# Attention: value pass in whole 512-column blocks instead of 256-column pieces, one block every second half step

## The reference, cut to what matters

```python
B, T, E = x.shape                      # 4, 1024, 128
q, k, v = ...                          # each (B, T, 16, 8); q and k are rotated
scores = jnp.einsum('bqhd,bkhd->bhqk', q, k) * scale
pages = jnp.arange(T) // PAGE_SIZE     # PAGE_SIZE = 32
allowed = pages[None, :] <= pages[:, None]
scores = jnp.where(allowed[None, None], scores, jnp.finfo(scores.dtype).min)
attn = jax.nn.softmax(scores, axis=-1)
out = jnp.einsum('bhqk,bkhd->bqhd', attn, v).reshape(B, T, E)
return out @ wo
```

## Time and profile before

| what | value |
|---|---|
| median of three runs | 1579.98 us |
| the profiled execution, its own time | 1579.82 us |
| its span in the profile | 1578.0 us |
| attention's value pass runs | from 142.0 us to about 486 us of the span |
| between 201.37 and 438.44 us: TensorE busy | 229.95 of 237.07 us |
| VectorE busy there | 232.91 us |
| ScalarE busy there | 221.52 us |

### The profile page before, as it was taken

One profiled execution on the slowest core, in us unless ns is written; L12 is line 12 of the kernel. 1 busy time (PEld: TensorE's weight loads), 2 busy tenths in 40 slices (PEclk: granted clock), 3 DMA queues, 4 the chain that ended last, 5 costly groups with the idle time before them and its releaser, 6 DMA issues. The chain is left out here.

```text
span 1578.0 us, 23831 instructions
## 1 busy us (share of the span) xinstructions
PE 1248.7 (79%) x7728; PEld 585.0 (37%) x7728; DVE 1171.5 (74%) x1342; ACT 727.4 (46%) x1121; POOL 506.3 (32%) x371
## 2 busy tenths in 40 slices
PE   4917999999985679999978767667666766666998
PEld 2402333333333534444533212222222222246565
DVE  5838999999954534444456789999999999984444
ACT  2504999999994143333336763323323323302221
POOL 2310001011002212233242256667666766622000
PEclk9956999999997579999988869999999999995999
DMA  3321111111104200000010022212212212100000
GB/s 89 137 74 36 64 45 54 51 56 57 37 21 118 68 0 1 0 0 0 0 27 0 4 69 80 79 58 76 80 66 76 70 66 80 53 1 27 14 13 27
DMA packets 45554, 74.01 MB, mean 47 GB/s; under 512 B 8983, under 2 KB 24999, under 8 KB 45479
## 3 DMA queue, kind: packets, MB, share of 16 engines
q1 hardware_dynamic: 44776, 72.26, 14.1%
q10 hardware_dynamic: 702, 0.73, 0.2%
HBM read 59.47 MB, written 13.11 MB: 46 GB/s over the span
## 5 line engine op out<-in xcount | busy, mean ns | idle before, releaser
L1586 POOL TENSOR_TENSOR ms_ch<-xnT,ms_c_rows 128x1024 f32<-128x1024 f32 x128 | 307.8, 2406 | 156.9 <-DVE xnT L1555 130.1
L611 DVE TENSOR_REDUCE att_found<-PS 128x2 f32<-128x1024 f32 (+2 forms) x288 | 333.4, 1219 | 19.9 <-PE PS L690 17.9
L666 ACT ACTIVATE att_prob<-PS 128x512 f32<-128x512 f32 x576 | 313.4, 596 | 28.3 <-PE PS L712 15.3
L1555 DVE TENSOR_TENSOR_SCAN xnT<-ms_decay,PS 128x1024 f32<-128x1024 f32 x128 | 285.2, 2269 | 0.0
L1533 ACT ACTIVATE ms_decay<-m_dt,m_a 128x1024 f32 x128 | 146.7, 1148 | 300.2 <-DVE xnT L1555 300.2
L1495 PE MATMUL PS<-ms_ch,ident_sb 128*128 128x512 f32 x512 | 265.3, 644 | 5.9 <-DVE m_u L1561 3.3
L1488 PE MATMUL PS<-m_bc,m_w_sel_b 96*128 96x512 bf16 (+1 forms) x256 | 83.9, 413 | 149.7 <-DVE xnT L1555 142.5
L731 PE MATMUL PS<-att_prob,att_v 128*32 128x256 f32 (+1 forms) x2560 | 182.2, 371 | 3.0 <-ACT att_out L655 2.8
L1550 DVE TENSOR_TENSOR PS<-ms_dtu,PS 128x1024 f32<-128x1024 f32 x128 | 150.9, 1215 | 16.0 <-PE PS L1488 15.6
L690 PE MATMUL PS<-kr,qr 55*128 55x128 bf16 (+4 forms) x1152 | 121.0, 291 | 41.4 <-DMA qr<-page_q 27.6
L1495 PEld LDWEIGHTS PS<-ms_ch,ident_sb 128*128 128x128 f32 x512 | 105.2, 207 | 101.8 <-issue 78.0
(11 more groups left out here) (209 smaller groups left out, 1594.1 us busy)
## 6 DMA issues: line engine op xcount, KB each, us to landing
ms_c_rows<-c_rows_dram SPq DMA_DIRECT2D x64, 512.0 KB, 3.6
qk_parts_dram<-qkv_parts SPq DMA_DIRECT2D x48, 128.0 KB, 1.8
heads_dram<-att_out SPq DMA_DIRECT2D x16, 256.0 KB, 2.5
qr<-qk_parts_dram SPq DMA_DIRECT2D x32, 96.0 KB
qr<-qk_parts_dram SPq DMA_DIRECT2D x96, 32.0 KB
kr<-qk_parts_dram SPq DMA_DIRECT2D x96, 32.0 KB
kr<-qk_parts_dram SPq DMA_DIRECT2D x32, 96.0 KB
X<-x SPq DMA_DIRECT2D x4, 512.0 KB, 6.0
```

What stands on the lines that cost most here:

```text
L611: dve.tensor_reduce(found[:, :, pair, first:first + (n - 1) * step + 1:step], PS[:, bank:bank + 2, :].rearrange("p r (w n) -> p r w n", w= ...
L666: act.activation(prob[:, step % PROB_RING * GH + h, :], PS[:, SCORE_BANK + unit % SCORE_RING, :], ACT.Exp, scale=float(D) ** -0.5).then_in ...
L1555: dve.tensor_tensor_scan(h[:, k, half, :], decay[:, k, half, :], inputs(half), 0.0, ALU.mult, ALU.add).then_inc(scanned, 1)
L1586: pool.tensor_tensor(ch[:, half, :], h[:, r % 2, half, :], c_rows[:, r, :], ALU.mult).then_inc(ch_ready, 1)
```

## The change

The pieces become whole blocks: 9 of 512 columns. Block v comes behind the scores of half step 2v + 4 (for v below 4) or 2v + 3.

```diff
@@ -448,7 +448,7 @@
 TURN_K = 7
-PIECE = 256
+PIECE = BANK
 NV = NK * BANK // PIECE
@@ -465,7 +465,7 @@
 def due(v):
 
-    return v + 4 if v < NV // 2 else v + 3
+    return 2 * v + 4 if v < NV // 2 else 2 * v + 3
```

## The result

The changed kernel takes 1624.8 us (median of four runs, 1619.9 to 1631.6) against 1580.2 for the kernel before on the same chip: a ratio of 1.0284, 95% interval 1.0238 to 1.0329. That is slower by 44.6 us; the forecast was 1622, 42 slower. Its profiled execution took 1628.7 us, with a span of 1626.9.

The account below looks back on a forecast made before the run. No engine was taken as full: TensorE, VectorE and ScalarE hand work to each other, with a ring floor of 1.08 us. About +2.8 us a group, 42.3 over the whole, took 1580.0 to 1622; range 1608 to 1633 for 8 in 10.

Parts of the forecast that it names:

- widening, nine half steps: Half steps going from one piece to two pieces' columns cost 0.43 us each, +3.87 a group; a vanishing wait gives -0.09.
- six emptied half steps: Half steps 0, 2, 5, 7, 9 and 16 lose their piece, falling only from 1.12 to 1.08 us: -0.24 a group.
- half step 12: It loses its double visit and falls from 1.55 to 1.08 us: -0.47 a group.
- half step 14: Without its piece the turn comes early, but ScalarE's copy waits behind an exponential: 1.60 to about 1.35 us, -0.25.
- behind the last turn: With no maxima left, 11 widened half steps cost +2.9 us and one losing a double visit gives -0.26: +2.6.
- first group: Half steps 4 to 7, at 1.2 GHz, cost +0.4 us; half steps 8 to 14 cost +1.0.
- the ring's floor: Scores wait for an earlier exponential in the ring of three banks, so no half step is shorter than 1.08 us.
- VectorE's floor: VectorE needs 21.2 us a group at most for 18 half steps, which no change of TensorE's order can pass.
- the bounds of the visit's length: A visit of 512 columns costs 0.86 to 1.14 us, taken as 1.00; 20 us either way in all.
- the first (TensorE's saved time counts): Faster: 8 fewer visits a group at 0.14 us, stopped by VectorE's 21.2 us, give 1574 us; chance 4%.
- The second: No change: empty half steps give back what long ones take, pairs of 2.24 us, 1580 us; chance 3%.
- The third: Slower still: TensorE's idles make the granted clock fall at times in the stage, eight falls, 1632 us; chance 8%.

Follow-up runs that it names:

- three pairs: The kernel before with pieces 2, 4 and 6 moved one half step later: 1603.8 us, ratio 1.0134.
- The old and the filled tail: Changed kernel, last two groups in the order before: 1618.5 us; or with unread maxima matmuls in those groups' half steps without a visit: 1627.7 us.
- copy first: Kernel with 18 spread pieces and early turn, plus the second group's copy DMAs moved ahead of the fourth group's row loads: 1579.1 us, ratio 0.9982.

## Why the prediction was right

Its range, direction and mechanism held, and the bulk of its sum did. The first four rows are the terms of one group and add up to the fifth; the last five rows above the sum are those of the whole stage. Both columns are differences of the changed kernel from the one before, the right one in the profiled executions:

| term | forecast, us | measured, us |
|---|---|---|
| widening, nine half steps | +3.87 - 0.09 = +3.78 | +3.73 |
| six emptied half steps | -0.24 | -0.19 |
| half step 12 | -0.47 | -0.41 |
| half step 14 | -0.25 | -0.21 |
| a group | +2.8 | +2.92 |
| twelve intervals of turns | 33.6 | 34.8 |
| second group | 2.2 | 2.2 |
| interval before the last turn | 2.5 | 2.6 |
| behind the last turn | 2.6 | 7.3 |
| first group | 1.4 | 2.4 |
| sum of the last five | 42.3 | 49.3 |

The span itself grew by 48.9 us: 0.7 us come before the first turn and about 1 less behind the last visit. That the median of 1624.8 lies within 3 us of the forecast of 1622 is partly luck. The profiled run has 6.6 us over my 42.3, and two of the four runs, 1619.9 and 1620.8, lie under the forecast.

The visit was read rightly from the double one, and the ring's floor from the single empty half step. A size was off: I took 1.08 us for every empty half step. The odd-numbered ones (3, 5, 7, 9) take 1.06 to 1.08, the even-numbered ones (0, 2, 12, 16) 1.12 to 1.14, and so do 6, 8 and 10 with three pairs. The difference lies between the scores and their exponential: it starts 0.42 us behind its scores in half step 5 (294.88 to 295.30) and 0.47 in half step 2 (290.88 to 291.35). Why isn't shown. It makes most of the 1.2 us between 33.6 and 34.8.

Two statements of the prediction were wrong without moving its number. VectorE's floor was 21.05 and not 21.2, as said above. And the bounds of the visit's length don't both stay in the range: by its own 20 us either way they give 1602 and 1642, and the range was 1608 to 1633. The measured 1.00 us kept this from mattering.

The rivals: the first (TensorE's saved time counts) needed empty half steps under 0.69 us, and they took 1.07. The time saved in the visits is real, though: one visit takes 1.00 us where two took 1.14. The Trainium skill, "TensorEngine Tiling (Array Packing)", Key Properties, says that a change of the tiling mode drains the engine, and this trace agrees in sign; no run tells how much of the 0.14 us is the drain. ScalarE's hold of the ring took this gain and more. The second needed a ring wait of 0.1 us; rows after an idle of ScalarE show 0.47.

The third was placed wrongly, and it is most of what the profiled run has over my sum. I asked for the clock in the stage, where it stays at 1.00 with TensorE 82% busy, and reasoned with that share. I had worked out the last group without maxima for its length and not for its share: 0.32 + 1.00 + 0.32 us in a pair of 2.42, some 68%. There the clock fell, for 13.7 us. So one sign that I had named for being wrong, a fall of the clock, did come, outside the stage that I had it watched in:

```profile
514.14 0.61 PE L712 MATMUL PS<-qr,kr 51*128 51x512 bf16 x2
515.44 0.61 PE L712 MATMUL PS<-qr,kr 51*128 51x512 bf16 x2 [0.69 <-ACT att_prob L666]
515.98 1.93 PE L731 MATMUL PS<-att_prob,att_v 128*32 128x512 f32 x8
517.85 0.61 PE L712 MATMUL PS<-qr,kr 51*128 51x512 bf16 x2
```

A pair of half steps takes 3.70 us there (514.14 to 517.85) instead of the 2.47 of this group at 1.00, so 13.7 x (1 - 2.47 / 3.70) = 4.6 us, which is about the 4.7 between 7.3 and 2.6.

The first group's extra 1.0 is the clock too: it rose at 154.2 us in the changed kernel and at 149.7 in the kernel before. This one is chance as far as the runs tell. The old and the filled tail have the same order in the first group, and there the clock rose at 149.4 and 149.3 us, and the first interval of turns took 25.92 and 25.88 us instead of 27.33.

## What to carry to other kernels

When several engines hand work to each other through a shallow ring, look for the shortest interval that the ring allows before work is bunched: time taken out of a step that is already at this floor is lost, and time put into its neighbour is paid in full. The trace of before may have one odd step of each kind, as here, and two such steps are worth more than any average. Look at the granted clock in every stretch that a change touches, the first group and the tail too, and compare intervals of turns before comparing totals: here the first group differed by 1.4 us between kernels with the same order in it.

## What the runs showed of the hardware

- The granted clock fell to 0.50 in the last group with TensorE busy 57 to 62% before it, in pieces of work 1.1 to 1.5 us apart and without one idle of 1 us. At about 80% in the same stretch it did not. Yet behind the same 2.10 us of work in 3.40 it fell in one profile and stayed at 1.00 in another. In the main stage it stayed at 1.00 with 82%.
- It also fell behind a single wait: for 3.4 us behind one of 2.66 us (1.44 us busy in 4.1), for 6.8 us behind one of 4.01 us.
- In the first group it rose to 1.00 anywhere from 149.3 to 154.2 us in four profiles with the same order there.
- A value visit costs the same in 16 matmuls of 256 columns as in 8 of 512: 1.00 us. Two separate visits of 256 cost 1.14.
- An interval of half steps that waits for an exponential of 512 columns took 1.06 to 1.14 us, and 0.85 to 0.93 with one of 256.
- SyncE's queue took about 12 us to send one group's loads (160.16 to 172.67, copy first), and a small DMA behind them went out only at 159.55 us, 3.4 us after ScalarE had its data ready (one piece in every half step).
